# Attention spreads alternate with weight loads, shared-expert pieces stand in the routing's waits, and the pair table's product runs on GpSimd

## What is computed

```
# L0: spectral mixing, eight blocks of 24 channels
Xf = fft2(x.reshape(B, H, W, C), norm='ortho')        # 9 of 16 columns carry all (real input)
o1 = relu(complex(Xf) @ w1 + b1)                       # per block, complex
o2 = softshrink(o1 @ w2 + b2, 0.01)
x  = irfft2(o2).reshape(B, C, H, W) + x
# L1: attention, 12 heads of 16, 4 x 256 tokens of 192
t  = tokens(x);  t = t + attn(layernorm(t)) @ w_proj + b_proj
# L1: mixture of experts
z  = layernorm(t)
shared = silu(z @ swg) * (z @ swu) @ swd
p, i = top_k(softmax(z @ w_gate + expert_bias), 2);  p = p / sum(p)
routed = sum over the two chosen experts e of p_e * (silu(z @ wg[e]) * (z @ wu[e])) @ wd[e]
out = t + shared + routed
```

## Time and profile before

| | us |
|---|---|
| median of 3 runs | 241.62 (239.68 to 241.91) |
| the profiled execution | 242.12, its span 240.3 |
| PE busy | 223.8 (93%) |
| DVE busy | 150.7 (63%) |
| ACT busy | 115.8 (48%) |
| GpSimd busy | 76.6 (32%) |
| PE in the chain that ended last | 77% of the span |
| mean granted clock of PE | 0.979 |

### The profile page before, as it was taken

How to read it: one execution, slowest core, us unless ns; L and a number is a source line. 1 busy time by engine, 2 the same in 40 slices (tenths; PEclk the granted TensorE clock), 3 DMA queues, 4 the chain that set the end, 5 groups by cost and what they waited for, 6 DMA issues and landing times.

```text
span 240.3 us, 5837 instructions
## 1 busy us (share of the span) xinstructions
PE 223.8 (93%) x1997; PEld 143.7 (60%) x1997; DVE 150.7 (63%) x355; ACT 115.8 (48%) x207; POOL 76.6 (32%) x119
## 2 busy tenths in 40 slices
PE   8799899954999999999899999999999999998994
PEld 3788666623566667677574664556565555553383
DVE  3446876640588897878767866565656565654252
ACT  0570163540355354434645357575757575746361
POOL 7030052000000082183510344465656565613000
PEclk9999999985799999999999999999999999999999
DMA  7871425998175995900740011111121111211434
GB/s 174 212 179 12 119 70 124 258 359 254 25 202 140 281 252 168 288 17 20 232 133 0 15 51 37 50 50 49 49 49 49 49 49 49 52 33 35 131 135 131
DMA packets 28115, 27.53 MB, mean 115 GB/s; under 512 B 7804, under 2 KB 26940, under 8 KB 28092
## 3 DMA queue, kind: packets, MB, share of 16 engines
q1 hardware_dynamic: 23276, 21.15, 32.4%
q0 software_dynamic: 2304, 4.72, 7.0%
q10 hardware_dynamic: 2512, 1.35, 1.9%
HBM read 22.34 MB, written 3.44 MB: 107 GB/s over the span
## 4 chain that ended last, share of the span: by engine, by line
PE 77%; SPq 11%; DMA 3%; issue 3%; ACT 2%; DVE 2%; DVEq 0%
PE grid L1581 11%; PE bank L1607 9%; PE grid L1339 8%; PE grid L1588 7%; PE bank L1597 4%; PE bank L1374 3%; PE grid L1473 3%; PE grid L1309 3%; PE bank L1357 3%; SPq L438 3%; PE bank L1261 2%; PE bank L1309 2%; DMA main<-main 2%; PE bank L1324 2%; PE grid L1478 2%
## 5 line engine op out<-in xcount | busy, mean ns | idle before, releaser
L763 ACT ACTIVATE main<-down_all 128x576 f32 x42 | 28.6, 684 | 27.4 <-PE bank L1607 26.2
L1086 DVE COPY main<-main 128x1152 f32 x41 | 31.6, 783 | 15.3 <-issue 13.7
L729 ACT ACTIVATE main<-grid 128x1024 f32<-128x1024 f32 x24 | 24.5, 1024 | 26.9 <-PE grid L1339 26.9
L595 POOL DMA_INDIRECT main<-xhat_rows,main x21 | 26.1, 1244 | 24.5 <-DVE main L1048 11.7
L1309 PE MATMUL grid<-main 32*128 32x256 f32 x132 | 28.2, 411 | 5.8 <-DMA main<-main 5.8
L1581 PE MATMUL grid<-main 128*64 128x384 f32 x160 | 29.8, 488 | 0.3 <-DVE main L1070 0.3
L603 POOL DMA_INDIRECT pair_rows<-main x19 | 20.4, 1073 | 25.9 <-DVE main L1076 25.9
L1339 PE MATMUL grid<-main 32*128 32x256 f32 x192 | 26.1, 399 | 0.9 <-ACT main L729 0.8
L900 DVE TENSOR_REDUCE main<-grid 128x2 f32<-128x512 f32 x33 | 21.8, 686 | 5.9 <-PE grid L1309 5.1
L1607 PEld LDWEIGHTS bank<-main 128*64 128x64 f32 x228 | 16.2, 136 | 12.3 <-ACT main L763 9.6
L1607 PE MATMUL bank<-main 128*64 128x192 f32 x228 | 22.7, 333 | 0.1
(11 more groups left out here) (213 smaller groups left out, 404.7 us busy)
## 6 DMA issues: line engine op xcount, KB each, us to landing
down_all<-wd SPq DMA_DIRECT2D x4, 1152.0 KB, 11.2
main<-wg SPq DMA_DIRECT2D x4, 576.0 KB, 4.4
main<-wu SPq DMA_DIRECT2D x4, 576.0 KB, 6.4
main<-wg SPq DMA_DIRECT2D x4, 288.0 KB, 7.0
main<-wu SPq DMA_DIRECT2D x4, 288.0 KB, 7.8
main<-main SPq DMA_DIRECT2D x8, 128.0 KB, 2.5
main<-x SPq DMA_DIRECT2D x1, 768.0 KB, 6.5
main<-wg SPq DMA_DIRECT2D x2, 384.0 KB, 4.3
```

Of the source, the lines that this page charges most:

```text
L595: pool.indirect_dma_start(xg[:, t % 2, :], None, xhat_rows, bass.IndirectOffsetOnAxis(ap=slot_token[:, t:t + 1].bitcast(U32), axis=0)).the ...
L729: act.activation(probs[:, quad % 2, 2 * (n % 2):2 * (n % 2) + 2, :, :].rearrange("p h k n -> p h (k n)"), grid[:, score_banks(n), :], ACT. ...
L763: act.activation(w_dn[:, p, h, :], dn_e(expert(t, h)), ACT.Copy).then_inc(S["w_dn_ready"], 1)
L1086: vec.tensor_copy(w_gu[:, p, h, :], gu_e(expert(t, h))).then_inc(S["w_gu_ready"], 1)
```

## The change

Five edits:
- `load_blocks` issues one half of a matrix (`k`). SP issues the second half of w1, then the second half of w2; ACT the first half of w1, the two biases of w1 (now counted by `ld_b1`), then the first half of w2. DVE negates w1 before its last copy of spectrum columns.
- In SP's queue down group 0 goes ahead of spread 0, and down group 1 behind spread 2. The wait for `tok_ready` goes.
- `keep_busy` is removed. Units 0 and 1 of the shared expert are cut into smaller pieces: the second image of unit 0 in two phases, unit 1 in a first-image phase 0, a second-image phase 0 (into the bank that the first opened, `opens=False`), and a common phase 1.
- The product `id_tile` moves from DVE to GpSimd, behind its last store of tokens; GpSimd waits for `is_tile_ready`, a new semaphore.
- DVE no longer waits for `is_tile` to end before `is_part`.

```diff
-        def load_blocks(queue, dst, src, sem):
-            for k in range(2):
...
+        def load_blocks(queue, dst, src, sem, k):
...
             sp.wait_ge(S["zeroed"], 3)
-            load_blocks(sp, w2, a["w2"], S["ld_w2"])
+            load_blocks(sp, w1, a["w1"], S["ld_w1"], 1)
+            load_blocks(sp, w2, a["w2"], S["ld_w2"], 1)
...
+            load_down(*DN_GROUPS[0])
             spread_rows(0)
             load_gate_up(*GU_GROUPS[0])
-            load_down(*DN_GROUPS[0])
-            sp.wait_ge(S["tok_ready"], B)
-            load_down(*DN_GROUPS[1])
             spread_rows(1)
             spread_rows(2)
+            load_down(*DN_GROUPS[1])
             load_gate_up(*GU_GROUPS[1])
...
+            pool.wait_ge(S["tables_ready"], 3)
+            pool.wait_ge(S["is_tile_ready"], 1)
+            nc.gpsimd.tensor_tensor(id_tile, is_tile, pair_id_h.unsqueeze(2).broadcast_to([128, NT * TOPK, 32]), ALU.mult).then_inc(S["id_tile_ready"], 1)
             pool.wait_ge(S["xhat2_stored"], 16 * NT)
...
             act.wait_ge(S["zeroed"], 5)
-            load_blocks(act, w1, a["w1"], S["ld_w1"])
+            load_blocks(act, w1, a["w1"], S["ld_w1"], 0)
...
+            load_blocks(act, w2, a["w2"], S["ld_w2"], 0)
...
-            act.wait_ge(S["ld_w1"], 10 * 16)
+            act.wait_ge(S["ld_b1"], 2 * 16)
...
                     fold(b + 2)
+                if b == B - 1:
+                    negate(w1, "ld_w1", 8)
                 spectrum_columns(b)
-            negate(w1, "ld_w1", 10)
             negate(w2, "ld_w2", 9)
...
-            step(vec.tensor_tensor(is_tile, first_slot_h.unsqueeze(1).broadcast_to([128, pairs, 32]),
-                                   base_h.unsqueeze(2).broadcast_to([128, pairs, 32]), ALU.is_equal))
-            vec.tensor_tensor(id_tile, is_tile, pair_id_h.unsqueeze(2).broadcast_to([128, pairs, 32]), ALU.mult).then_inc(S["id_tile_ready"], 1)
+            vec.tensor_tensor(is_tile, first_slot_h.unsqueeze(1).broadcast_to([128, pairs, 32]),
+                              base_h.unsqueeze(2).broadcast_to([128, pairs, 32]), ALU.is_equal).then_inc(S["is_tile_ready"], 1)
...
             gate_logits(2)
             tokens_for_experts(3)
-            keep_busy(3)
+            shared_gate_up(0, second, range(0, 1))
             gate_logits(3)
-            shared_gate_up(0, second, range(0, 1))
-            keep_busy(2)
+            shared_gate_up(0, second, range(1, 2))
+            shared_gate_up(1, first, range(0, 1))
             rank_and_count()
-            shared_gate_up(0, second, range(1, 2))
+            shared_gate_up(1, second, range(0, 1), opens=False)
             base()
-            shared_gate_up(1)
+            shared_gate_up(1, range(2), range(1, 2))
```

More of the change, by code:

```diff
@@ L298, in program @@
         bank = [grid[:, i, :] for i in range(QUAD)] + [ctx.enter_context(nc.psum_tensor(f"bank{i}", [128, 512], F32)) for i in range(QUAD, 8)]
-        names = """idle_set folded_ready ld_fwd ld_const ld_w1 ld_w2 ld_res ld_attn ld_qkv ld_shared ld_gu ld_dn
+        names = """idle_set folded_ready ld_fwd ld_const ld_w1 ld_b1 ld_w2 ld_res ld_attn ld_qkv ld_shared ld_gu ld_dn
         zeroed w_zeroed w_spread filled eps_set negated
@@ L307, in program @@
         stats2 mv2 refined std2 rstd2 xhat2_ready xhat2_last xhat2_stored x2T_done x2T_ready
-        logits_done gap_ready other_ready route member_ready tables_ready rank_done count_done base_done end_done inv_done
+        logits_done gap_ready other_ready route member_ready tables_ready rank_done count_done base_done is_tile_ready end_done inv_done
         padded_ready ended_ready is_part_ready id_tile_ready experts_done expert_ready used_ready loop_act loop_dve pair_ready slot_pair_ready scattered slot_token_ready
@@ L408, in load_pixels @@
                             a["x"][b].rearrange("c h w -> (c h w)").rearrange("(k p c) -> p k c", k=2, p=128)).then_inc(ld_pix[b], 16)
-        def load_blocks(queue, dst, src, sem):
-            for k in range(2):
[L413 to L418, removed]
+        def load_blocks(queue, dst, src, sem, k):
+            i, o = slice(BLK * k, BLK * k + BLK), slice(BLK * k, BLK * k + BLK)
+            im = slice(IM + BLK * k, IM + BLK * k + BLK)
+            block_k = src.rearrange("r (q k) i o -> k r i q o", k=2)[k]
+            for r in range(2):
+                queue.dma_start(dst[i, :, r, o], block_k[r]).then_inc(sem, 16)
+                queue.dma_start(dst[im, :, 1 - r, o], block_k[r]).then_inc(sem, 16)
         @block.sync
@@ L643, in _ @@
             act.wait_ge(S["zeroed"], 5)
-            load_blocks(act, w1, a["w1"], S["ld_w1"])
+            load_blocks(act, w1, a["w1"], S["ld_w1"], 0)
             with nc.allow_non_contiguous_dma(reason="a bias per channel"):
                 for r in range(2):
-                    act.dma_start(b1[IM * r:IM * r + GC, :], a["b1"][r].rearrange("n o -> (n o)").rearrange("(q p) -> p q", p=GC)).then_inc(S["ld_w1"], 16)
+                    act.dma_start(b1[IM * r:IM * r + GC, :], a["b1"][r].rearrange("n o -> (n o)").rearrange("(q p) -> p q", p=GC)).then_inc(S["ld_b1"], 16)
+            load_blocks(act, w2, a["w2"], S["ld_w2"], 0)
             for b in range(B):
@@ L1465, in _, with shared_gate_up @@
                     gate_logits(0)
-            def shared_gate_up(u, images=range(2), phases=range(2)):
+            def shared_gate_up(u, images=range(2), phases=range(2), opens=True):
                 half, f = u // FC, u % FC
@@ L1473, in shared_gate_up @@
                         mm(bank[shared_banks(u)[m]][:, cols], shared_gu[:, m * FF + 128 * f:m * FF + 128 * f + 128],
-                           x2T[:, batch, m, :], start=True, stop=False)
+                           x2T[:, batch, m, :], start=opens, stop=False, skip_group_check=(u == 1))
                 if 1 in phases:
@@ L1478, in shared_gate_up @@
                         last = mm(bank[shared_banks(u)[m]][:, cols], shared_gu[rows, 2 * FF + 128 * f:2 * FF + 128 * f + 128],
-                                  x2T[rows, batch, 1 - m, :], start=False, stop=True)
+                                  x2T[rows, batch, 1 - m, :], start=False, stop=True, skip_group_check=(u == 1))
                         if images.stop == 2:
@@ L1517, in slot_tokens @@
                 last.then_inc(S["inv_done"], 1)
-            def keep_busy(n):
-                for _ in range(n):
-                    mm(bank[0][:, 0:512].rearrange("p (a n) -> p a n", a=4), ones, ones.unsqueeze(1).broadcast_to([128, 4, 128]), start=True, stop=True)
             def tile_experts():
```

## The result

| | before | changed |
|---|---|---|
| median, us | 241.47 (239.68 to 241.91, 4 runs) | 235.06 (233.69 to 239.83, 4 runs) |
| the same, measured again | 241.18 | 234.76 (234.37 to 235.58, 6 runs) |
| ratio, 95% interval | | 0.9724 [0.9663, 0.9786]; again 0.9737 [0.9706, 0.9769] |
| span of a profiled execution | 240.3 | 232.9 |

The time forecast was 234.5. The ratios leave out executions that a lower clock set apart from the others.

A forecast was written before the change was run, and what follows sets the result against it. The prediction took TensorE's serial chain as the bound, stalled by a late SBUF-to-SBUF spread. Gain 8.5 less 1.3 for a later `slot_tokens` gave 7.2; 241.6 - 7.2 = 234.4, said as 234.5, range 232.5 to 237.6.

The forecast's parts named there:

- attention: In attention's start: SP's new order removes PE's 5.81 wait and the slow clock behind it, 8.5 faster.
- start: At the kernel's start: PE's 1.31 wait goes, but waits for the last bias grow; nothing gained, 0.59 at most.
- pieces in the routing, until `base`: In the routing: shared-expert pieces replace five fillers ahead of `base`; DVE's chain is 0.8 late at worst.
- product on GpSimd, against DVE: Before `slot_tokens`: DVE saves 0.61, but GpSimd's product, run only after `is_part`, costs 1.2.
- clock behind `slot_tokens`: Rival, chance 0.20: the clock falls at PE's longer wait before `slot_tokens`; 2.9 lost at most, 1.5 if it returns sooner.
- a clock under 1.00 after `slot_tokens`: Sign of being wrong: granted clock under 1.00 around 25 or after `slot_tokens`; two wrong signs would spoil the number.
- the stated range: Whole kernel: 232.5 (hidden product less 0.3%) to 237.6 (one lost clock with the product run after `is_part`).
- The mechanism: In SP's queue: spread 1 issued near 41.5, landing by 48.5 at the latest, before PE asks at 51.27.
- the stall: In attention's start: PE stood still 5.81, 51.27 to 57.08, for spread 1, then ran at 1.2 GHz until about 62.85.
- The rival: Chance 0.20: clock falls at a new PE wait, near 24 or before `slot_tokens`; 2.9 lost at most, 236 to 237.4.
- the two bounds of the product: Before `slot_tokens`: 0 if GpSimd's product hides beside `is_part`, 1.2 if it runs only after; 1.2 taken.
- the serial product: Before `slot_tokens`: GpSimd's product runs only after `is_part`, costing 1.2; PE's wait there 2.6 instead of 1.4.

The follow-up runs named there:

- a1: The changed kernel itself, measured and profiled again, against the kernel before: 234.76, ratio 0.9737, profiled span 232.9.
- e1: The kernel before with SP's new queue order alone; measured twice: 232.42 (0.9636) and 233.31 (0.9678).
- e7: The kernel before with SP's new order and the start's edit, routing and product as before: 232.92, ratio 0.9649.
- e2: The changed kernel with SP's order and its wait for `tok_ready` as before: 243.91 (240.47 to 249.9), ratio 1.0022.
- e3: The changed kernel with the product `id_tile` back on DVE, pieces and start as changed: 235.06, ratio 0.9749.
- e8: The changed kernel with twenty matmuls of ones ahead of `slot_tokens`: 233.94, ratio 0.9695.
- e4: The changed kernel with the start's edit undone (w1 and w2 loads, negation of w1 as before): 235.59, ratio 0.9767.
- e9: The changed kernel with start and product as before, the last shared unit's second half moved ahead of `slot_tokens`: 233.37, ratio 0.9682.
- e10: The kernel before with SP's new order, plus bases right behind the ranks and `is_part` in two halves: 232.7, ratio 0.9654.
- e5: The changed kernel with DVE waiting for GpSimd's product before `is_part`, so nothing runs beside it; one execution, 235.58.

## Why the prediction was right, and where its terms were off

The median came out 0.3 to 0.6 from the forecast, but as a sum of errors that cancel. By the landmarks of a1:

| term | predicted | read |
|---|---|---|
| attention | -8.5 | -9.5 (80.5, that is 117.2 - 36.7, to 71.0) |
| start | 0 | 0, with a risk seen in two executions |
| pieces in the routing, until `base` | at most 0.8 late | +0.6 (11.6, that is 128.8 - 117.2, to 12.2) |
| product on GpSimd, against DVE | +1.2 - 0.61 | +0.26 |
| clock behind `slot_tokens` | a rival, not in the sum | +1.5 |
| sum | -7.2 | -7.1 |

The spans differ by 7.4; the rest is the 0.3 by which a1's first `pair_for_max` is early. That the sum met the forecast is luck in part: attention gave 1.0 more and the product cost 0.3 less than forecast, which paid for a fall of the clock that the sum left out. Of the signs named in the prediction, a clock under 1.00 after `slot_tokens`, a sign of being wrong, shows in a1; in the first profile it shows there and near 25, and that execution, 239.83, lies above the stated range.

**The spreads.** The mechanism held in every step: nothing held at SP's queue, copies landed in 2.4 in the median, clock 1.00, no later spread late. By this pair of profiles the term was 0.9 to 1.0 too small. I had priced the work behind the stall at full clock from its own rows: half of 2.08 for the four pairs of `pair_for_max`, then 0.37 for the transposes. But in a1 those matmuls (L1312) run beside the scores of unit 3 (L1342), the two lines taking turns in the timeline: the rows above end the last `pair_for_max` at 51.12 and start the projection (L1264) at 51.33, 0.35 after the scores' end at 50.98 (50.57 + 0.41), and that with the transposes in between. I had allowed 1.04 + 0.37 = 1.41. The stall had not only cost its wait and its clock, it had also pulled apart two loops that otherwise overlap. The scores of unit 4 start at 62.57 before, by the timeline, and at 52.92 in a1; less the 0.3 of a1's earlier start that is 9.35, the measured term. The profiled execution of the kernel before has a mean clock of 0.979, while most of its others have 0.984 to 0.986, so they lost less to the low clock; the medians of e1 gave 8.8 and 7.8, on either side of the 8.5 forecast.

**The start.** Right that it gains nothing: PE's wait of 1.31 before w1 is gone (w1's matmuls start at 9.58 in a1, 10.29 before), but DVE then waits for the last bias, 2.46 in a1 and 3.65 in the first profile (3.4 forecast), and PE waits for DVE, 0.93 in a1, 1.01 in e7, 2.12 in the first profile (1.9 forecast):

```profile
24.14 0.75 DVE L869 COPY main<-main 128x64 f32<-128x64 f32 x4 [3.65 <-DMA v_bias<-b_qkv]
...
26.32 0.47 PE L1217 MATMUL grid<-cf,main 128*128 128x128 f32 x1 [2.12 <-DVE main L877]
```

```profile
26.00:27.00 1.00, 0.68 (x3) 0.68 (x4) 0.73 (x2) 0.00 (x0) 0.00 (x0) 0.50 0.24 66
30.00:34.00 4.00, 4.00 (x19) 3.04 (x18) 1.93 (x6) 0.00 (x0) 0.00 (x0) 0.50 0.82 246
36.20:36.40 0.20, 0.20 (x4) 0.20 (x3) 0.00 (x0) 0.20 (x1) 0.00 (x0) 0.88 0.03 8
```

Both fences are of the first profile, the timeline and then three windows. The clock fell at about 26.0, shortly before that wait ended, and was at 0.50 until about 36.2; the first `pair_for_max` started at 41.3 instead of 36.4. That is the execution of 239.83. The rival had this place in view and priced it at 2.9 at most, from the one low stretch of the profile before. Here the delay is 4.9: 0.8 by the later end of the wait (26.32 against 25.49 in a1), and 4.1 behind it, since the stretch was some 10 us long. The profile of e2, which has the changed start too, shows the same fall after a shorter wait, in the timeline and three windows:

```profile
25.75 1.43 PE L1218 MATMUL grid<-cf,main 128*128 128x128 f32 x6 [1.58 <-DVE main L878]
```

```profile
25.80:26.00 0.20, 0.20 (x2) 0.20 (x3) 0.20 (x1) 0.00 (x0) 0.00 (x0) 0.81 0.34 77
26.00:28.00 2.00, 2.00 (x12) 1.50 (x12) 0.78 (x3) 0.98 (x2) 0.00 (x0) 0.50 0.36 60
29.00:30.00 1.00, 1.00 (x12) 0.79 (x11) 0.70 (x3) 0.23 (x1) 0.00 (x0) 0.83 0.53 146
```

There the clock was back after 3.4 us, and the first `pair_for_max` started at 37.9. So the clock fell at this place in two of the seven profiles with the changed start (waits of 0.63 to 2.12), and in none of the six with the start as before (waits of 0.59 at most). The times say the same less surely. In e7 one of six executions took 237.49, 4.6 above its median; where in it the clock fell no profile shows. Of the 28 executions of the changed kernel, a1, e3, e7 and e8 these two are so far out, of the 30 with the start as before (e1 twice, e4, e9, e10) none. In e2 the stall spreads the times as well, up to 249.9. That is a strong hint that the start edit adds this risk, not a proof.

**The pieces and the product.** `base` comes 0.6 later relative to attention's end, inside the 0.8. The choice between the two bounds of the product was right: it is serialised, as L889 was and not as L935. The Trainium skill, SBUF — State Buffer, "Who interferes with whom", says that the port pair shared by DVE and GpSimd is an exclusive lock, and that a DVE instruction with two SBUF inputs contends with a GpSimd instruction that reads SBUF; that whoever issues first gets the pair for the whole instruction it says of DVE's 2-port modes. The 2.94 beside and 1.04 alone agree with such a lock. The term was a little too large: my 1.2 held a start and a signal that were behind the product already when `is_part` let it go, so it ended 0.90 after it. Against a product on DVE the loss is 0.26, and the whole delay of `slot_tokens`, counted from attention's end, is 0.8 (16.9 before, 17.7 in a1), not 1.3. No run has the new pieces alone, so their 0.6 is read from the landmarks and not tested by itself.

**The clock.** This was the rival, given 0.20, and by the mean clocks it happened in nearly every execution of the changed kernel: PE waits 2.43 before `slot_tokens`, and the clock falls soon after it resumes. The prediction put this wait where fillers had stood; they had stood before the count, and it was the useful work behind `base` that had been moved away. The price, 8.38 - 6.84 = 1.5, is the smaller of the two that the rival had (1.5 and 2.9). Two executions with a mean clock of 1.00 are known, 233.69 of the changed kernel and 233.84 of e4; they lie where e8 lies, 233.47 to 234.44, as they should. What failed is the chance, not the mechanism. The wait that spared the clock had lasted 1.31; the one that the forecast itself contained, 2.6 with the serial product, was twice as long, and should have counted with the stall. If the fall had been in the sum with the terms as I had them, the forecast would have been 235.9 (241.6 - 7.2 + 1.5); with the terms as read it is 234.5 (241.6 - 7.1), the number forecast.

**What stays open.** The runs don't settle why the low stretch lasted 3.4 us in one place and some 10 in another, nor how often the changed start costs up to 5 us. Nor do they settle why the undone spreads cost only about 6 in the quickest executions of e2 (240.7 against 234.8), where the profiles of e1 and a1 give 9.4. Part of it may be that a1 had lost 1.5 to the clock behind `slot_tokens`, and that these executions, at a mean clock of 0.986, perhaps had not; no profile of one was taken. What a mended start edit would be worth was not tried.

## What to carry to other kernels

When a transfer stalls TensorE, price the removal by the distance between the last instruction before the stall and the first one well behind it in an undisturbed neighbour, not by the wait and the rows behind it: overlap of small matmuls is lost too, and reappears. Before fillers are replaced by useful work, ask what wait opens where that work had stood; a wait of 2.4 us left empty cost 1.5 us by the slow clock here, and twenty matmuls of ones took that away. Useful work moved into the wait kept the clock in five of six executions (e9), but left PE waiting behind it. And a change of several edits is worth splitting on the chip: one of the five brought 8.8 and 7.8 in two measurements, and the others together gave 2.3 and 1.4 of it back.

## What the runs showed of the hardware that was not expected

- A GpSimd product of 512 fp16 columns takes 1.04 alone (e5) and 2.94 beside a VectorE comparison of 2.28 with two SBUF inputs (a1); the comparison lost nothing. The one that began first went on undisturbed and the other bore the whole cost.
- The length of a wait alone does not tell whether the clock falls. It fell with waits of 2.83 (e5), 2.43 (a1), 2.17 (e3), 2.12 (first profile) and 1.58 (e2), and held after 1.72 (e5) and 1.59 (e8), both at the start, and after 1.31, 1.09 (e9) and 1.01 (e7). It fell during the wait (first profile, near 26), 0.6 after PE had resumed (a1) and 2.0 after it (e5, behind `slot_tokens`). It came back 3.4 us after it fell in a1 and some 10 after it in the first profile.
- Where the clock can fall in several places, one kernel's executions lay 9 us apart (e2, 240.47 to 249.9, by mean clock 0.986 down to 0.952). In the profiled one, 244.44, it was low three times: from about 25.9, from 56.7 and from 135.2.
